# A two-layer graph kernel: the order of high parts, x loads, packing and joins

## What is computed

```
Wh = x @ W                                     # 8192 x 128
e  = leaky_relu((Wh @ a1)[:, None] + (Wh @ a2)[None, :], 0.2)
att = softmax(where(adj > 0, e, -9e15), axis=1)
x1 = layernorm(x + elu(att @ Wh))
m  = (adj @ x1) / adj.sum(axis=1, keepdims=True)
out = layernorm(x1 + concat([m, x1]) @ weight + bias)
```

## Time and profile before

| | us |
|---|---|
| median of three runs | 1609.38 (1608.64 to 1609.53) |
| profiled execution | 1609.33 |
| its span, first to last instruction | 1607.4 |
| PE busy | 1495.1 (93%) |
| PEld busy | 1298.3 (81%) |
| DVE busy | 983.8 (61%) |
| ACT busy | 970.5 (60%) |
| POOL busy | 116.9 (7%) |

### The profile page before, as it was taken

One profiled execution on the slowest core, in us unless ns is written; L12 is line 12 of the kernel. 1 busy time (PEld: TensorE's weight loads), 2 busy tenths in 40 slices (PEclk: granted clock), 3 DMA queues, 4 the chain that ended last, 5 costly groups with the idle time before them and its releaser, 6 DMA issues.

```text
span 1607.4 us, 38356 instructions
## 1 busy us (share of the span) xinstructions
PE 1495.1 (93%) x13894; PEld 1298.3 (81%) x13894; DVE 983.8 (61%) x2786; ACT 970.5 (60%) x2384; POOL 116.9 (7%) x199
## 2 busy tenths in 40 slices
PE   6487998999999899989999999998999999999998
PEld 6366787888888788878878888887888888888886
DVE  7986576677767767767777677664443444344343
ACT  3797789998988899899989888980100000010000
POOL 1001010001001000100010010000000000000000
PEclk9698999999999999999999999999999999999999
DMA  9957968867775787687677755013000000000000
GB/s 169 114 56 82 105 71 91 87 79 78 89 89 71 85 90 85 70 91 87 79 78 89 89 71 69 14 48 100 17 20 16 16 16 16 16 16 20 16 16 16
DMA packets 99714, 101.59 MB, mean 63 GB/s; under 512 B 4704, under 2 KB 66912, under 8 KB 99680
## 3 DMA queue, kind: packets, MB, share of 16 engines
q0 software_dynamic: 33792, 67.11, 42.0%
q1 hardware_dynamic: 65888, 34.03, 8.2%
HBM read 289.77 MB, written 12.68 MB: 188 GB/s over the span
## 4 chain that ended last, share of the span: by engine, by line
PE 33%; ACT 30%; DVE 24%; issue 9%; DMA 1%; ACTq 1%; DVEq 1%; SPq 0%; POOL 0%; POOLq 0%
PE acc L691 29%; ACT level_ring L424 27%; DVE edge_ring L895 5%; DVE level_ring L888 4%; DVE adj_space L839 2%; PE turn_ps L715 2%; PE acc L617 2%; DVE edge_ring L830 2%; ACT part_sums L435 1%; DVE adj_space L842 1%; DVE words L817 1%; DVE rows_y L987 1%; ACT words L403 1%; DVE row_sums L930 1%; DVE row_sums L938 1%
## 5 line engine op out<-in xcount | busy, mean ns | idle before, releaser
L424 ACT ACTIVATE level_ring<-s_row,cols 128x256 fp8e4<-128x256 f32 x2048 | 832.2, 498 | 0.0
L617 PE MATMUL acc<-factors,edge_ring 128*128 128x258 f16 x4096 | 558.0, 276 | 59.0 <-ACT part_sums L435 50.2
L617 PE MATMUL acc<-factors,level_ring 128*128 128x258 f16 x4096 | 558.2, 276 | 8.0 <-DVE row_sums L917 8.0
L691 PE MATMUL acc<-factors,adj_space 128*128 128x258 f16 x4096 | 469.4, 273 | 4.5 <-issue 4.5
L617 PEld LDWEIGHTS acc<-factors,edge_ring 128*128 128x128 fp8e4 x4096 | 367.5, 98 | 120.7 <-issue 64.6
L691 PEld LDWEIGHTS acc<-factors,adj_space 128*128 128x128 fp8e4 x4096 | 399.3, 97 | 63.6 <-issue 4.7
L617 PEld LDWEIGHTS acc<-factors,level_ring 128*128 128x128 fp8e4 x4096 | 367.8, 98 | 65.4 <-issue 8.3
L888 DVE TENSOR_TENSOR level_ring<-level_ring,edge_ring 128x1024 uint16<-128x1024 uint16 x256 | 174.2, 691 | 185.6 <-ACT level_ring L424 174.7
L581 PE MATMUL pack_ps<-pack_w,adj_space 128*128 128x32 bf16 x1024 | 172.4, 177 | 23.3 <-DVE adj_space L842 23.3
L522 ACT ACTIVATE part_sums<-acc 128x258 f32<-128x258 f32 x32 | 12.4, 386 | 297.4 <-PE acc L691 297.4
L895 DVE TENSOR_TENSOR edge_ring<-edge_ring,level_ring 128x1024 uint16<-128x1024 uint16 x256 | 166.7, 684 | 0.0
(11 more groups left out here) (92 smaller groups left out, 729.8 us busy)
## 6 DMA issues: line engine op xcount, KB each, us to landing
adj_space<-in_adj POOLq DMA_DIRECT2D x64, 1024.0 KB, 15.5
x_parts<-parts SPq DMA_DIRECT2D x32, 129.0 KB, 2.9
factors<-x_parts SPq DMA_DIRECT2D x8, 516.0 KB, 6.8
factors<-in_x SPq DMA_DIRECT2D x8, 512.0 KB, 7.2
s_row<-s_and_t SPq DMA_DIRECT2D x32, 128.0 KB, 2.9
rows_x<-in_x SPq DMA_DIRECT2D x32, 128.0 KB, 3.0
x_rows<-rows_y SPq DMA_DIRECT2D x32, 128.0 KB, 9.8
rows_x<-x_rows SPq DMA_DIRECT2D x32, 128.0 KB, 2.1
```

What stands on the lines that cost most here:

```text
L424: a = act.activation(level_bytes[:, h % MASK_SLOTS, j, :], s_row[:, slot, :], ACT.Relu, bias=t_big[:, h * HALF + j:h * HALF + j + 1], scal ...
L617: m = pe.matmul(acc[a][:, 0:ROW], mask, factors[:, neg, jj, :], start=(jj == 0), stop=(jj == NJ - 1))
L691: m = pe.matmul(acc[b][:, 0:ROW], ring_1_bytes[:, c, j, b * P:(b + 1) * P], factors[:, 0, jj, :], start=(jj == 0), stop=(jj == NJ - 1))
```

## The change

- `high_parts` of group g - 2 moves on ScalarE from behind h = 1 to behind h = 4 of group g, so behind the positive copy.
- SP issues `load_x(g)` ahead of `store_x1(g - 1)`, not behind it.
- The first 512 rows aren't joined. TensorE packs them from the raw bytes: `pack_bits` takes four matmuls for each 128 columns, one for each row tile, in accumulation, with four sets of weights (`pack_w` times 1, 2, 4, 8), which VectorE makes with three more small instructions.
- The joins of block 1 stood all in group 1 and those of block 2 in groups 2 and 3. Now groups 1, 2 and 3 have 3, 3 and 2 joins of these eight, and the packs and word copies follow. From block 3 on the order is as it was.

```diff
@@ -89,7 +89,7 @@
         consts_sb = sb("consts_sb", [P, P + WPT], F32)
-        pack_w = sb("pack_w", [P, WPR], BF16)
+        pack_w = sb("pack_w", [P, TILES, WPR], BF16)
         s_row = sb("s_row", [P, 2, GROUP], F32)
@@ -267,8 +267,8 @@
                 if not first:
+                    load_x(g)
                     store_x1(g - 1)
-                    load_x(g)
@@ -456,10 +456,10 @@
                         act.wait_ge(f_low_ok, UPG)
-                    if h == 1 and not second:
-                        high_parts(g - 2, before_last)
                     if h == 2:
                         copy_positive(g - 1, second)
+                    if h == UPG and not second:
+                        high_parts(g - 2, before_last)
                     if h % 2 and h // 2 in next_words:
@@ -484,9 +484,9 @@
                     act.activation(v_col, vy_col, ACT.Exp).then_inc(exp_cols_ok, 1)
-            group(1, 1, 1, {2: (1, 0), 3: (1, 1)}, second=True)
-            group(2, 0, 2, {0: (1, 2), 1: (1, 3), 3: (2, 0)}, before_last=True)
-            group(3, 1, 2, {1: (2, 1), 3: (2, 2)})
+            group(1, 1, 1, {3: (1, 0)}, second=True)
+            group(2, 0, 2, {0: (1, 1), 1: (1, 2), 3: (1, 3)}, before_last=True)
+            group(3, 1, 2, {0: (2, 0), 1: (2, 1), 3: (2, 2)})
             with act.Fori(2, NR - 1) as n:
@@ -570,20 +570,25 @@
-            def packable(n, c, first=False):
-                pe.wait_ge(joined_ok, UPG * n + c + 1)
-                if not first:
-                    pe.wait_ge(words_ok, UPG * n + c - 1)
+            def packable(n, c):
+                pe.wait_ge(joined_ok, UPG * (n - 1) + c + 1)
+                pe.wait_ge(words_ok, UPG * n + c - 1)
...
                 nibbles = adj_ring[:, c, 0, j * P:(j + 1) * P].bitcast(F8)
-                return pe.matmul(pack_ps[c % 2][:, j * WPR:(j + 1) * WPR], nibbles, pack_w[:, :], start=True, stop=True)
-
-            def pack(c):
-
+                return pe.matmul(pack_ps[c % 2][:, j * WPR:(j + 1) * WPR], nibbles, pack_w[:, 0, :], start=True, stop=True)
+
+            def pack_bits(c):
+
+                pe.wait_ge(adj_in[c], 16)
+                if c >= 2:
+                    pe.wait_ge(words_ok, c - 1)
                 for j in range(UNIT):
-                    m = pack_tile(c, j)
+                    for t in range(TILES):
+                        bits = adj_ring[:, c, t, j * P:(j + 1) * P].bitcast(F8)
+                        m = pe.matmul(pack_ps[c % 2][:, j * WPR:(j + 1) * WPR], bits, pack_w[:, t, :],
+                                      start=(t == 0), stop=(t == TILES - 1))
                 m.then_inc(packed, 1)
@@ -595,9 +600,8 @@
             pe.matmul(turn_ps[1][:, 0:F], sum_xb, wq[:, 0:F], start=True, stop=True).then_inc(mean_made, 1)
-            pe.wait_ge(pack_w_ok, TILES)
-            packable(0, 0, first=True)
-            pack(0)
+            pe.wait_ge(pack_w_ok, 2 * TILES - 1)
+            pack_bits(0)
@@ -625,10 +629,10 @@
-            def group(g, n, packs):
+            def group(g, packs):
                 for c in range(UPG):
                     for h in (2 * c, 2 * c + 1):
-                        pack_chunk = packs.get(c) if h % 2 else None
+                        n, pack_chunk = packs.get(c, (0, None)) if h % 2 else (0, None)
                         if pack_chunk is not None:
@@ -636,16 +640,17 @@
                 if c < UPG - 1:
-                    packable(0, c + 1, first=(c == 0))
-                    pack(c + 1)
+                    pack_bits(c + 1)
                 for h in (2 * c, 2 * c + 1):
                     multiply(0, h, h % 2 == 0, True)
-            group(1, 1, {c: c for c in range(UPG)})
-            with pe.Fori(1, NR - 1) as n:
-                group(PAIR * n, n + 1, {1: 0, 3: 1})
-                group(PAIR * n + 1, n + 1, {1: 2, 3: 3})
-            group(NG - 2, NR, {})
-            group(NG - 1, NR, {})
+            group(1, {1: (1, 0), 2: (1, 1), 3: (1, 2)})
+            group(2, {1: (1, 3), 2: (2, 0), 3: (2, 1)})
+            group(3, {1: (2, 2), 3: (2, 3)})
+            with pe.Fori(2, NR - 1) as n:
+                group(PAIR * n, {1: (n + 1, 0), 3: (n + 1, 1)})
+                group(PAIR * n + 1, {1: (n + 1, 2), 3: (n + 1, 3)})
+            group(NG - 2, {})
+            group(NG - 1, {})
@@ -746,10 +751,13 @@
                     dve.wait_ge(pack_w_ok, i)
-                    dve.scalar_tensor_tensor(out=pack_w[:, :], in0=digit, scalar=weight, in1=pack_w[:, :],
+                    dve.scalar_tensor_tensor(out=pack_w[:, 0, :], in0=digit, scalar=weight, in1=pack_w[:, 0, :],
                                              op0=ALU.mult, op1=ALU.add).then_inc(pack_w_ok, 1)
                 else:
-                    dve.tensor_scalar(pack_w[:, :], digit, weight, None, ALU.mult).then_inc(pack_w_ok, 1)
+                    dve.tensor_scalar(pack_w[:, 0, :], digit, weight, None, ALU.mult).then_inc(pack_w_ok, 1)
+            dve.wait_ge(pack_w_ok, TILES)
+            for t in range(1, TILES):
+                dve.tensor_scalar(pack_w[:, t, :], pack_w[:, 0, :], 2.0 ** t, None, ALU.mult).then_inc(pack_w_ok, 1)
@@ -838,14 +846,13 @@
                                          op0=ALU.logical_shift_left, op1=ALU.bitwise_or).then_inc(joined_tiles, 1)
-                dve.wait_ge(joined_tiles, UPG * n + c + 1)
+                dve.wait_ge(joined_tiles, UPG * (n - 1) + c + 1)
                 dve.scalar_tensor_tensor(out=joined[:, c, 0, :], in0=joined[:, c, TPG, :], scalar=TPG,
...
             make_product(1)
-            join(0, 0)
             dve.tensor_scalar(y_col, s_col, t_max, None, ALU.add).then_inc(y_ok_col, 1)
@@ -993,19 +1000,19 @@
                     normalise(g - 2, rstd_ok, x1_ok)
-                for c in joins.get(0, ()):
-                    join(n + 1, c)
+                if 0 in joins:
+                    join(*joins[0])
                 masks(n, q, 1, "sums", second)
-                for c in joins.get(1, ()):
-                    join(n + 1, c)
+                if 1 in joins:
+                    join(*joins[1])
                 masks(n, q, 2, "softmax")
...
                     low_parts(g - 2)
-                for c in joins.get(2, ()):
-                    join(n + 1, c)
+                if 2 in joins:
+                    join(*joins[2])
                 masks(n, q, 3)
-                for c in joins.get(3, ()):
-                    join(n + 1, c)
+                if 3 in joins:
+                    join(*joins[3])
                 elu_and_residual(g - 1, second)
@@ -1014,7 +1021,6 @@
                     make_product(2 * c + 3)
-                    join(0, c + 1)
                 masks(0, 0, c)
@@ -1022,10 +1028,12 @@
             dve.wait_ge(one_row_ok, 1)
-            group(0, 1, {c: (c,) for c in range(UPG)}, second=True)
-            with dve.Fori(1, NR - 1) as n:
-                group(n, 0, {0: (0,), 3: (1,)})
-                group(n, 1, {0: (2,), 3: (3,)})
+            group(0, 1, {0: (1, 0), 1: (1, 1), 2: (1, 2)}, second=True)
+            group(1, 0, {0: (1, 3), 2: (2, 0), 3: (2, 1)})
+            group(1, 1, {0: (2, 2), 3: (2, 3)})
+            with dve.Fori(2, NR - 1) as n:
+                group(n, 0, {0: (n + 1, 0), 3: (n + 1, 1)})
+                group(n, 1, {0: (n + 1, 2), 3: (n + 1, 3)})
             group(NR - 1, 0, {})
...
             normalise(NG - 2, rstd_ok, x1_ok)
```

## The result

| | before | changed |
|---|---|---|
| median of 4 runs, us | 1609.01 (1608.12 to 1609.53) | 1529.78 (1528.94 to 1531.69) |
| profiled execution, us | 1609.33 | 1531.69 |
| its span | 1607.4 | 1530.0 |
| PE busy | 1495.1 (93%) | 1480.1 (97%) |
| DVE busy | 983.8 (61%) | 980.3 (64%) |

The changed kernel takes 0.951 of the time before, 95% interval 0.9493 to 0.9526: 79 us less. The forecast was 1530, with 1523 to 1546 as its range.

What follows compares the result with a forecast made beforehand. A ring through ScalarE's wait for normalised rows bounds the loop; freed, TensorE does. 103.2 + 59.7 + 792.7 + 57.2 + 0.2 = 1013.0, then 514.7 untouched and 1.93 around the span: 1530, range 1523 to 1546.

Steps and rivals of the forecast that it cites:

- The ring of 31.58 us through L448: Layer 0's loop: h = 7 scores, 10.2 us of VectorE, then ScalarE's wait at the high parts set 31.58 per group.
- 59.5 + 1.9 = 61.4 in the sum: Gain from moving the high parts: 59.5 us in groups 3 to 29, 1.9 in groups 30 and 31.
- TensorE's 29.36: TensorE's own time per loop group with two packed chunks, drain taken off; forecast as the new period, 29.36 us.
- The reserves: Spare time per loop group: VectorE 0.9 us (negative sum at T + 28.9, T being TensorE's start), ScalarE 1.1.
- small hand-overs stay: Rival: 0.5 to 1 us per group boundary remains in the loop, giving 1544 to 1557; chance 0.09.
- Clock dips: Loop's six half-clock losses of 1.5 us go with the idle; rival that they stay: 1539, chance 0.04.
- Part 2: x load issued ahead of the x1 store; removes VectorE's 8.61 us stand before the residual at 171.89.
- part 4: Joins 3, 3, 2 in groups 1 to 3 remove the 11.22 us idle at 144.21; gain 15.5 up to group 3.
- Part 3: Raw packing of the first 512 rows, 1.8 us per chunk; group 1 starts at 103.2 for 106.19.
- Behind layer 0: What follows layer 0, 514.7 us, was forecast as untouched.
- slower: Rival: the x1 store, behind the x load, lands late; at 27 us each group takes 33.5, time 1641; chance 0.02.
- a ring of the same length: Rival: another ring inherits the wait at the high parts, the loop keeps 31.58 per group, time 1589; chance 0.03.

Runs made afterwards that it cites:

- three tiny activations: The changed kernel with three 128x4 activations, each waiting for the one before, added behind the high parts of every group on ScalarE: 1533.6 us, ratio 0.9529.
- part 3 undone: The changed kernel with the first 512 rows joined by VectorE again and packed with one matmul per 128 columns: 1532.3 us, ratio 0.9526.
- part 2 undone: The changed kernel with the x load issued behind the x1 store again: 1539.6 us, ratio 0.9572.

## Why the prediction was right

- *The bound.* The ring of 31.58 us through L448, with TensorE idle inside it, was read rightly: the high parts' place alone is worth 61 us (59.5 + 1.9 = 61.4 in the sum).
- *TensorE's 29.36.* Measured 29.39. Taking off the drain of 0.16 mattered: without it the sum would have been 4 us too high over 27 groups.
- *The reserves.* ScalarE's 1.1 is measured as 1.05 of waiting, and as 1.2 between the two periods (29.39 and 28.22). VectorE was forecast at the negative sum at T + 28.9: the group that starts at 486.8 has it at 515.49, T + 28.7, and the next one, where VectorE stands 0.5 at L838, at 545.36, T + 29.2. So its reserve is not 0.9 throughout but some 1.1 and 0.6 in turn, and the three tiny activations used up the smaller one. In the changed kernel the rival "small hand-overs stay" has nothing: no wait of TensorE is listed and 27 groups take 29.39 each.
- *Clock dips.* They went with the idle: no window of 10 us between 90 and 1010 is below 1.00, where the kernel before had six dips in the loop; with the high parts put back they returned, one every fourth group. This is what the rule of the Trainium skill that the prediction names ("TensorE: Matmul & The Clock Gate", Part 1) would make of it, and the trace agrees. That rival is out for this loop. One reading behind it was wrong: the 28 boundaries did not have much the same gap. In the trace of the kernel before twelve had 2.32 or 2.33 us, seven had 1.77, and the rest less; the dips came after every second one of the twelve.
- *Part 2* was priced together with part 4 only (15.5; measured 15.6). That sum came from the measured 75.2 and so held the slower matmuls behind the stalls. Taken apart, part 2 is worth 9.8 and part 4 11.2 (8.1 and 9.4 by the profiled spans), together more than 15.6, so they overlap. The separate estimate for part 2, 6 to 7, left the half clock out.
- *Part 3.* Raw packing was taken at 1.8 us per chunk against a bound of 7.1: measured 1.75, by start and end of 64 matmuls. The gain at group 1 was forecast as 3.0 and is 2.3; the score row arrived at 51.29 for 50.34, a term that I had held fixed. It came anywhere between 49.05 and 51.29 in the traces of kernels that load it alike. Counted from its arrival, group 1 starts after 52.6 us for 55.9 before, 3.3 less, and after 56.3 with part 3 undone.
- *Behind layer 0* I had taken no change, and it took 1.1 us more. The change isn't shown to be the cause: in the traces of kernels that don't differ there this stretch took 514.6 to 517.6.
- *The other rivals.* The x1 stores land in at most 10.4 us between 200 and 1000, so "slower" is out; a ring of the same length is out by the period, alone (no wait of TensorE) and together.

The forecast's nearness to the last tenth is partly luck. For the profiled execution it was 1529.6, and that took 1531.7: 0.7 more at the start, 0.2 less in groups 1 and 2, 0.7 more from group 3 to the end of layer 0, 1.1 more behind it, and 0.2 less around the span. The median happened to lie 1.9 below that execution.

## What to carry to other kernels

When an engine that is nearly full waits a little in every iteration, follow that wait back through the engines until it comes round to itself; the period is the ring's, not any engine's, and moving one small waiting instruction behind more ready work opens it. Before trusting the new period, work out every engine's own time per iteration and its position at each hand-over: here reserves of 0.6 to 1.2 us decided that nothing was left of the ring, and adding or removing work by design measured them. Work them out for every kind of group: the smallest one counts. Where a stall stops TensorE, count the slower matmuls after it too.

## What the runs showed of the hardware

- After 4.33 us of idling TensorE ran at 0.50 for several us (part 2 undone). In the loop of the kernel before it fell to 0.50 after 6 of 12 gaps of 2.32 or 2.33 us, every second one, and after none of seven gaps of 1.77. After 3.24 us, before slice h = 6 of group 0 in the changed kernel, at 95.34, it stayed at 1.00; the same gap stands at 93.89 with three tiny activations and at 93.73 (3.21 us) with the high parts behind h = 2, and there the mean from 90 to 100 was 0.83 and 0.66. The length of the gap alone doesn't tell it in these traces.
- 64 matmuls of 32 columns with a new 128x128 weight each, four in accumulation, take 1.75 us at full clock, 27 ns each, and 1.89 at 44.5 us, where the clock was 0.50: 30 ns each.
- A 128 KB x load, whose median from issue to landing is 3.0 us in the kernel before and 2.1 in the changed one, took 15.3 us beside queued adjacency chunks, in two kernels alike (156.53 in the earlier trace rows, 147.4 with part 2 undone).
